# Two attention stages: diagonal blocks cleared by GpSimd in the first, four heads side by side with sums by GpSimd in the second

## The reference

```python
# layer 0 (latent keys and values, 8 values per head, 32 shared rotary rows); layer 1 (latent of 32, no rotary)
scores = q @ k.T * scale              # per batch and head, 1024 x 1024
scores = where(key <= query, scores, -inf)
probs = exp(scores - max) / sum(exp(scores - max))
x = x + (probs @ v) @ W_o
```

## Time and profile before

| | us |
|---|---|
| median of 3 runs | 3160.7 |
| lowest, highest | 3154.9, 3165.1 |
| the profiled execution | 3168.4 |
| span of its trace | 3166.7 |

### The profile page before, as it was taken

The page is one execution under the profiler, slowest core; times in us unless marked ns, Lnnn a source line. Parts: engine busy times, 40 slices in busy tenths (PEclk is TensorE's granted clock), DMA queues, the critical chain, the costliest instruction groups (busy, mean ns, idle before and its releaser), DMA issues. The chain is left out here.

```text
span 3166.7 us, 46665 instructions
## 1 busy us (share of the span) xinstructions
PE 2361.7 (75%) x13512; PEld 1225.4 (39%) x13512; DVE 1743.7 (55%) x5508; ACT 1241.0 (39%) x1983; POOL 488.8 (15%) x524
## 2 busy tenths in 40 slices
PE   4559999999956328866999999999677292877382
PEld 1114344343334126532443434444254271554262
DVE  4656666666344886265665655666365324576223
ACT  2405455555534644553444444444222141343141
POOL 1400000000003000032000000000043463033554
PEclk9759999999977659877999999999888596988686
DMA  4272444443030000233122121121120152000144
GB/s 130 76 144 45 86 76 85 86 85 60 11 103 3 1 8 28 64 110 109 44 57 54 45 55 42 48 64 37 60 83 21 52 142 81 3 4 15 40 138 129
DMA packets 177903, 199.81 MB, mean 63 GB/s; under 512 B 36384, under 2 KB 117920, under 8 KB 177568
## 3 DMA queue, kind: packets, MB, share of 16 engines
q1 hardware_dynamic: 160000, 173.72, 22.1%
q0 software_dynamic: 9216, 19.02, 1.8%
q10 hardware_dynamic: 8448, 4.20, 0.4%
HBM read 127.09 MB, written 69.76 MB: 62 GB/s over the span
## 5 line engine op out<-in xcount | busy, mean ns | idle before, releaser
L910 ACT ACTIVATE at_probs<-at_score 128x1024 f32<-128x1024 f32 (+7 forms) x1024 | 655.2, 652 | 872.8 <-PE at_score L835 539.1
L935 DVE CUSTOM_DVE_ANT_0 at_masked<-at_mx,g_maskw 128x512 bf16<-128x512 f32 (+3 forms) x1024 | 483.4, 486 | 180.9 <-PE at_mx L801 177.6
L801 PE MATMUL at_mx<-at_K,at_Q 96*128 96x512 bf16 (+7 forms) x1536 | 467.0, 344 | 119.0 <-DVE at_mpart L935 40.9
L833 PE MATMUL at_score<-at_Q,at_K 96*128 96x512 bf16 (+7 forms) x1536 | 504.1, 332 | 28.9 <-issue 14.3
L835 PE MATMUL at_score<-at_Q,at_K 98*128 98x512 bf16 (+7 forms) x1536 | 507.2, 331 | 0.0
L931 DVE TENSOR_REDUCE at_mpart<-at_mx 128x1 f32<-128x512 f32 x512 | 353.8, 691 | 265.3 <-PE at_mx L801 245.1
L855 PE MATMUL at_outp<-at_probs,at_vop 128*32 128x512 f32 (+6 forms) x3072 | 445.2, 497 | 0.0
L801 PEld LDWEIGHTS at_mx<-at_K,at_Q 120*128 120x128 bf16 (+1 forms) x1536 | 148.4, 98 | 440.3 <-DVE at_mpart L935 198.6
L833 PEld LDWEIGHTS at_score<-at_Q,at_K 120*128 120x128 bf16 (+1 forms) x1536 | 149.8, 98 | 339.3 <-issue 183.1
L1025 POOL MEMSET n_spread<- 16x128 f32 (+1 forms) x2 | 0.7, 356 | 1541.0 <-POOLq L636 1541.0
L838 PE MATMUL at_score<-g_maskkq,g_identb 128*128 128x128 bf16 x1024 | 225.3, 220 | 0.0
(11 more groups left out here) (467 smaller groups left out, 3408.6 us busy)
## 6 DMA issues: line engine op xcount, KB each, us to landing
at_Q<-q SPq DMA_DIRECT2D x192, 128.0 KB, 3.0
at_Q<-qr SPq DMA_DIRECT2D x72, 256.0 KB, 5.9
at_K<-kr SPq DMA_DIRECT2D x72, 256.0 KB, 6.9
q<-p_pieces SPq DMA_DIRECT2D x40, 384.0 KB, 3.3
at_K<-k SPq DMA_DIRECT2D x168, 64.0 KB, 2.1
buf<-g_zeros SPq DMA_DIRECT2D x32, 325.0 KB, 5.0
o<-at_osb SPq DMA_DIRECT2D x64, 128.0 KB
n_oc<-o SPq DMA_DIRECT2D x8, 1024.0 KB, 5.0
```

Of the source, the lines that this page charges most:

```text
L801: pe.matmul(bank[:, 0:hi - lo], Q0[0:R, g % 4, j, qt * P:(qt + 1) * P], K0[0:R, g % 4, j % KG, lo:hi], start=True, stop=True).then_inc(s_m ...
L833: pe.matmul(bank, K0[0:R0, g % 4, j % KG, kb * P:(kb + 1) * P], Q0[0:R0, g % 4, j, lo:hi], start=True, stop=False)
L910: act.activation(probs[:, kb % 2, j, kb * P:T], src, ACT.Exp, scale=cf.scale).then_inc(s_exp, 1)
L935: dve.tensor_tensor_reduce(masked[:, u % 2, 0:w], mx[:, u % 2, 0:w], k.maskw[:, CH - w:CH], 1.0, NEG, ALU.add, ALU.max, mpart[:, part, j, ...
```

## The change

For both stages: `Cfg` gets `clear_probs` (true in the first attention) and `pool_sums` (true where `d == M`, which is the second attention with its new `G=4, M=32`).

First attention: TensorE no longer adds the mask to the diagonal block. GpSimd sets the entries above the diagonal of each 128x128 diagonal block of `probs` to zero after the exponential, and `values` waits for that.

Second attention: 16 steps of 4 heads in place of 32 of 2. The values fill all 32 columns, so there is no column of ones. GpSimd adds the `probs` of key blocks 0 to 6 in f32 into `acc` (24 additions and one that copies, per step), `probs` becomes a ring of 3, and TensorE multiplies `acc` and the last block with ones into the two `mx` banks at the step's end (`sums`), from which VectorE copies them to `lsb`. The mask of the second attention stays on TensorE.

```diff
+        self.clear_probs = bool(SR)
+        self.pool_sums = d == M
...
-    MU = 12 * G + 2
+    MU = 12 * G + SU + 2
+    NBP = 3 if SUMS else 2
+    ADDED = 6
...
+        def add_probs(b, g):
+            pool = nc.gpsimd
+            n = b * GN + g
+            for kb in range(1, ADDED + 1):
+                for j in range(G):
+                    pool.wait_ge(s_exp, n * U + kb * G + j + 3)
+                    if kb == 1 and j == 0:
+                        pool.wait_ge(s_mx, earlier_sums(b, g))
+                        pool.tensor_tensor(acc[:, :, 0:P], probs[:, 0, :, 0:P],
+                                           k.zeros[:, 0:G * P].rearrange("p (j t) -> p j t", t=P), ALU.add).then_inc(s_acc, 1)
+                    if kb > 1:
+                        pool.wait_ge(s_acc, added(n, kb - 1, j))
+                    so_far = probs[:, 0, j, P:T] if kb == 1 else acc[:, j, kb * P:T]
+                    pool.tensor_tensor(acc[:, j, kb * P:T], so_far, probs[:, kb % NBP, j, kb * P:T],
+                                       ALU.add).then_inc(s_acc, 1)
...
+            def clear_diagonals(b, g):
+                n = b * GN + g
+                for kb in range(QT):
+                    for j in range(G):
+                        part = probs[:, kb % NBP, j, kb * P:(kb + 1) * P]
+                        pool.wait_ge(s_exp, n * U + kb * G + j + 3)
+                        pool.sem_inc(s_ppassed, 1)
+                        pool.affine_select(out=part, in_=part, compare_op=ALU.is_ge, fill=0.0, base=0,
+                                           pattern=[[1, P]], channel_multiplier=-1).then_inc(s_dg, 1)
...
-                    diag = lo == kb * P
+                    diag = lo == kb * P and not cf.clear_probs
...
+                if cf.clear_probs:
+                    pe.wait_ge(s_dg, n * U + (kb + 1) * G)
...
+            def sums(b, g):
+                u = sum_at(b, g)
+                pe.wait_ge(s_acc, added(b * GN + g, ADDED, G - 1))
+                for half in range(2):
+                    pe.wait_ge(s_mxf, u + half + 1)
+                    for j in range(G):
+                        out = mx[M * j:M * (j + 1), half, :]
+                        last = pe.matmul(out, ones[:], acc[:, j, half * CH:(half + 1) * CH], start=True, stop=(half == 0))
+                    if half == 1:
+                        for j in range(G):
+                            last = pe.matmul(mx[M * j:M * (j + 1), half, CH - P:CH], ones[:],
+                                             probs[:, (QT - 1) % NBP, j, T - P:T], start=False, stop=True)
+                    last.then_inc(s_mx, 1)
...
-                    act.wait_ge(s_pv, n * 8 + kb - 1 + NPC)
+                    act.wait_ge(s_pv, n * 8 + (kb - 1 if kb < 2 or not SUMS else max(kb - 2, 0)) + NPC)
...
+                        if SUMS and kb == 0:
+                            act.wait_ge(s_acc, added(n - 1, ADDED, j))
+                        if SUMS and kb >= 3:
+                            act.wait_ge(s_acc, added(n, max(kb - 3, 1), j))
...
+                for half in range(2 if SUMS else 0):
+                    dve.wait_ge(s_mx, sum_at(b, g) + half + 1)
+                    dve.tensor_copy(lsb[:, g % 2, half * CH:(half + 1) * CH], mx[:, half, :]).then_inc(s_mxf, 1)
...
-        cf = Cfg(G=2, M=64, HR=0, SR=0, d=LD, scale=0.125, k_per_head=False)
+        cf = Cfg(G=4, M=32, HR=0, SR=0, d=LD, scale=0.125, k_per_head=False)
```

More of the change, by code:

```diff
@@ L628, in attention @@
     U = QT * G
-    MU = 12 * G + 2
+    SUMS = cf.pool_sums
+    SU = 2 if SUMS else 0
+    MU = 12 * G + SU + 2
+    NBP = 3 if SUMS else 2
+    ADDED = 6
+    AU = 1 + ADDED * G
     NARROW = {5: [3], 6: [2, 1], 7: [0]}
@@ L648, in attention @@
         osb = c.sb("osb", [P, 2, T])
+        if SUMS:
+            acc = c.sb("acc", [P, G, T])
+            ones = c.sb("ones", [P, 32])
+            lsb = c.sb("lsb", [P, 2, T])
         masked = c.sb("masked", [P, 2, CH], BF16)
@@ L663, in attention @@
         s_ms, s_passed = c.sem("shift_stored"), c.sem("sync_passed")
-        s_dpassed = c.sem("vector_passed")
+        s_dpassed, s_ppassed = c.sem("vector_passed"), c.sem("pool_passed")
+        s_dg = c.sem("diagonal_cleared")
+        s_acc = c.sem("probs_added")
+        STORES = 2 if SUMS else G + 1
         block = st.enter_context(nc.Block())
@@ L703, in ahead, with sum_at, earlier_sums, added @@
             return b, g
+        def sum_at(b, g):
+            n = b * GN + g
+            if ahead(b, g, 2):
+                return (n + 2) * MU + SUM_U
+            return NB * GN * MU + (2 if g == GN - 1 else 0)
+        def earlier_sums(b, g):
+            n = b * GN + g
+            if ahead(b, g, 1):
+                return (n + 1) * MU + SUM_U + 2
+            return NB * GN * MU + 2
+        def added(n, kb, j):
+            return (n + 1) * AU + 1 + (kb - 1) * G + j + 1
         def over_batches(eng, step):
@@ L752, in store @@
                 wait(s_oev, b * GN + g + 2)
+                if SUMS:
+                    sp.dma_start(o_scr[ds(g * G * d, G * d), ds(first_token(b), T)], osb[:, g % 2, :]).then_inc(s_os[g % 2], 16)
+                    wait(s_mxf, sum_at(b, g) + 4)
+                    sp.dma_start(l_scr[ds(g * G, G), ds(first_token(b), T)],
+                                 lsb[0:(G - 1) * M + 1:M, g % 2, :]).then_inc(s_os[g % 2], 16)
+                    return
                 for j in range(G):
@@ L783, in _ @@
             pool.memset(K1[SHIFT_ROW:SHIFT_ROW + 2, :, :, :], 1.0).then_inc(s_set, 1)
+            if SUMS:
+                pool.wait_ge(s_set, 1)
+                pool.memset(ones[:], 1.0).then_inc(s_set, 2)
+                pool.sem_inc(s_acc, AU)
+                over_batches(pool, add_probs)
+                return
             pool.wait_ge(s_set, 1)
@@ L804, in max_units, with turn_max @@
                 return u
-            def turn_max(b, g, u):
+            def turn_max(b, g, u, off=0):
                 n = b * GN + g
@@ L893, in step @@
                 values(b, g, QT - 1)
+                if SUMS:
+                    sums(b, g)
             over_batches(pe, step)
@@ L916, in _, with reduce_units @@
         def _(dve):
-            dve.sem_inc(s_mxf, 2)
+            dve.sem_inc(s_mxf, 2 + 2 * SU)
             dve.sem_inc(s_oev, 1)
-            dve.sem_inc(s_os[0], 16 * (G + 1))
-            dve.sem_inc(s_os[1], 16 * (G + 1))
-            def reduce_units(b, g, parts, u):
+            dve.sem_inc(s_os[0], 16 * STORES)
+            dve.sem_inc(s_os[1], 16 * STORES)
+            def reduce_units(b, g, parts, u, off=0):
                 n = b * GN + g
@@ L939, in reduce_units, with finish_max @@
                 return u
-            def finish_max(b, g, u):
+            def finish_max(b, g, u, off):
                 n = b * GN + g
-                dve.wait_ge(s_mxf, n * MU + u + 2)
+                dve.wait_ge(s_mxf, n * MU + u + 2 + off)
                 dve.tensor_tensor(mpart[:, 0, :, 4:8], mpart[:, 0, :, 4:8], mpart[:, 1, :, 4:8], ALU.max).then_inc(s_mc, 1)
@@ L962, in copy_turned, with wide_maxima @@
                     u += 1
-            def wide_maxima(b, g):
-                u = reduce_units(b, g, WIDE, NARROW_U)
-                finish_max(b, g, u)
-                copy_turned(b, g, u)
+            def wide_maxima(b, g, off=0):
+                u = reduce_units(b, g, WIDE, WIDE_AT, off)
+                finish_max(b, g, u, off)
+                copy_turned(b, g, u, off)
             def values(b, g):
@@ L975, in _ @@
             values(0, 0)
-            reduce_units(0, 0, NARROW, 0)
-            wide_maxima(0, 0)
-            reduce_units(0, 1, NARROW, 0)
+            reduce_units(0, 0, NARROW, 0, 2 * SU)
+            wide_maxima(0, 0, SU)
+            reduce_units(0, 1, NARROW, 0, SU)
             def step(b, g):
```

45 lines of the change are left out of this document (28 added, 17 removed).

## The result

| | before | changed kernel |
|---|---|---|
| median | 3160.9 us | 3237.8 us (3221.9 to 3247.3) |
| ratio, 95% interval | | 1.0238 (1.0218 to 1.0259), slower |
| profiled execution, span | 3166.7 us | 3245.5 us |
| first exponential to end of last copy, first attention | 646.3 us | 645.0 us |
| the same, second attention (with the copies of the sums) | 786.6 us | 845.0 us |

The account below looks back on a forecast made before the run. TensorE, helped by VectorE, was taken to set the pace. Second attention -40.2 us and first -8 us bring 3168.4 us to 3120 profiled, 3112 us as median; 8-in-10 range 3065 to 3165 us.

Parts of the forecast that it names:

- What GpSimd does to VectorE: Second attention: GpSimd's additions block `finish_max`, stalling TensorE 2.8 us in each of 15 steps, 42 us.
- the forecast's picture: In `finish_max`, the first instruction waits for the rest of one addition, the three others for a whole one: 5.6 us.
- Steps as in the first attention: Second attention: its 16 steps take the first attention's 646.3 us in place of 786.6, a gain of 140.3 us.
- sums on TensorE 2.1 us: Second attention, step's end: the products with ones cost 2.1 us in each of 16 steps, 33.6 us.
- lead-in: Before the second attention's first score: maxima of twice the heads cost 21.3 us more, longer query loads 1.8 us.
- Does GpSimd keep up?: Second attention: GpSimd's additions take 32.4 us a step at 2.26 ns a column, about level with TensorE.
- the upper row: GpSimd's additions: five in a row took 6.06 us, 2.37 ns a column, which would give 33.9 us a step.
- 0.5 us late at the most: Second attention: without the stall, GpSimd's additions end at most 0.5 us after TensorE's last values of a step.
- First attention, -8 us: First attention: dropping the mask products saves 0.5 us a step, 8 us, with 0 and 28 as ends; clearing costs nothing.
- no contention: Rival, second attention: VectorE's tiny instructions slip in between additions, saving the 42 us; 3078 us, chance 0.17.
- GpSimd is the bound and the kernel gets slower: Rival, second attention: TensorE waits at `sums` for the last addition; up to 3211 us at the slowest row, chance 0.25.
- The forecast's own test: Changed trace: TensorE idle ahead of `sums` means wrong price per column; idle at neither `sums` nor `turn_max`, wrong contention.

Follow-up runs that it names:

- filled stall: Changed kernel with 36 products of 512 columns, results unread, on TensorE ahead of its wait for `finish_max`; 3218.0 us, ratio 1.0182.
- thin additions: Changed kernel with each of GpSimd's 24 additions of a step cut to its first 32 columns; 3081.1 us (one execution).
- PSUM form: Changed kernel with `finish_max` as three instructions, the first a reduction, in place of four, intermediate values in a free PSUM bank; 3121.5 us, ratio 0.9869.
- second part alone: Changed kernel without the clearing: first attention's mask stays a product on TensorE, only the second attention is changed; 3233.9 us, ratio 1.0216.
- halved additions: Changed kernel with each of GpSimd's 24 additions of a step cut into two instructions of half the columns; 3282.1 us (one execution).
- the maximum with its result in PSUM: Changed kernel with `finish_max` in three instructions through PSUM, the first a maximum of two SBUF operands in place of a reduction; 3225.7 us (one execution).

## Why the prediction was wrong

**The step that failed is the one headed "What GpSimd does to VectorE", and in it the length of the wait.** Who blocks whom is right: `finish_max` is blocked by GpSimd's additions, since its operands lie in SBUF, and TensorE idles ahead of `turn_max`. The moment is right too (chain 23.9 us into the step, forecast 24.0), and in one chain of 15 so is the size. But the first instruction was priced at the rest of one addition, 0.45 us, with 3.8 us as the upper bound of the whole stall; in 14 chains of 15 it waited 10.4 us, for the end of GpSimd's run. The term is 15 x 2.8 = 42 us, and 117.0 were measured.

The rows that it rested on the earlier trace rows are true, and the trace before has more of their kind. In it VectorE instructions with two SBUF operands were held while another addition was still to come, and all 20 got in at the first boundary: 12 L460 (six of them in runs of two additions, as in rows 9, six in runs of five), and 8 L1293. VectorE in the run of five of rows 6, then the third, fourth and fifth of its additions:

```profile
1376.13 1.48 DVE L1293 TENSOR_TENSOR p_rest<-p_lat,p_pieces 32x512 f32<-32x512 f32 x1 [0.32 <-ACT p_pieces L1249]
...
1377.93 0.72 DVE L460 SCALAR_TENSOR_TENSOR p_shift<-p_mv,p_rstd 128x4 f32<-128x4 f32 x1
```

```profile
1375.91 1.16 POOL L1309 TENSOR_TENSOR p_pieces<-p_rest,p_pieces 128x512 bf16<-128x512 f32 x1
1377.03 1.60 POOL L1309 TENSOR_TENSOR p_pieces<-p_rest,p_pieces 128x512 bf16<-128x512 f32 x1
1378.59 1.14 POOL L1309 TENSOR_TENSOR p_pieces<-p_rest,p_pieces 32x512 bf16<-32x512 f32 x1
```

L1293 has 0.94 us of the third addition in front of it, about what L1055 has of its own, and gets in behind it; the fourth addition is held in turn (1.60 us). L460 gets in behind the fourth. So the old trace spoke for the forecast's picture, and the fault was to take what held in one stage for a bound in another. What makes the difference is open. A bound from the other side was to be had: whatever stands in front of GpSimd without waiting for this chain, which is the rest of block 3 (0.9 + 3 x 1.5 us) and block 4 (4 x 1.22), 10.3 us.

The 121.7 us that are missing in the second attention:

| term | forecast | measured | from |
|---|---|---|---|
| stall ahead of `turn_max` | 42 | 117 | waits of the changed kernel |
| clock behind the stall | 0 | 20 to 35 | filled stall: difference of the medians, and 14 held steps x 2.5 us |
| GpSimd's tail in the last step | 0 | about 11 | last copy of the sums 9.3 us behind the copy-out, 1.9 with thin additions; that copy-out 34.0 us after the step's first exponential, 30.1 with them (ScalarE waits 6.0 us for GpSimd in that step, 1.3 with them) |
| sum of the differences | | 106 to 121 of 122 | |

What is left, 1 to 16 us, I did not take apart.

- *Steps as in the first attention, sums on TensorE 2.1 us, lead-in:* right. Last values to next scores take 2.05 us; from the first L877 to the first exponential it is 46.5 us, 21.5 more than before, forecast 21.3 and 1.8.
- *The clock* is missing from the forecast altogether, though it knew of a stall. Even the stall of the forecast's size, 2.67 us, was followed by slower products (L911 with 384 columns 0.53 us, 0.33 at the full clock, in the rows above), and its step is 5.1 us longer than the same one with thin additions (50.5 against 45.5 us, both at the turn of the loop). This alone would have made 42 us some 76.
- *Does GpSimd keep up?* Not quite: it works from 6.85 to 40.85 us into an undisturbed step, 34.0 us or 2.37 ns a column, where I took 2.26. That this is the price of the upper row is chance: the 6.06 us there hold the 0.45 us by which the fourth addition was held. The others start 1.12 us apart, and additions of 512 columns with f32 operands 1.22 us, so with f32 operands, named as the open part, an addition costs some 9% more. TensorE's values end at 39.5. "0.5 us late at the most" was 0.4 to 1.9 us in 14 steps of the PSUM form and 5.0 and 5.6 us in the last two. In the changed kernel the stall covers this, as the forecast said; without the stall it is the next limit (29.1 us of waits; the second attention of the PSUM form takes 721.5 us, with thin additions 678.3).
- *First attention, -8 us:* wrong, and with the other sign; measured +3.5 us (+0.6 to +6.3). Plain steps do get 0.2 to 0.6 us shorter (40.1 and 40.0 in place of 40.3 and 40.6), but VectorE's reductions take the place of the product. A few steps are 1 us longer in some executions (with a dip of the clock in them), and the two at the turn of the loop 0.6 us (46.7 in place of 46.1).
- *The rivals:* "no contention" (3078) is what the thin additions give (3081), but it wasn't the case here. "GpSimd is the bound and the kernel gets slower" had the right sign and engine but the wrong path: the time is lost at `turn_max`, not at `sums`. The forecast's own test said so in advance: idle time at `turn_max` speaks for contention, at `sums` for the price.

## What to carry to other kernels

Before GpSimd is given long work in a row, list VectorE's instructions in that stretch with two SBUF inputs or with a copy or scaling from SBUF to SBUF, and bound the wait of each by the whole of GpSimd's queue, not by one instruction. A chain on the critical path can be written with reductions and a PSUM end instead; here that cost nothing. Price a stall of TensorE with the half-speed stretch behind it. And a wait seen in one stage, even 20 times of 20, is a size and not a bound for another: put the worst case that the instruction order allows beside it.

## What the runs showed of the hardware

- In the second attention a blocked VectorE instruction is mostly held for the whole back-to-back run of GpSimd: 10.4 us over seven boundaries between additions, 12.6 us over more than twice as many of half the length. It either gets in at the first boundary (1.0 us) or at none: of 75 first links with two SBUF sources in five kernels (the changed one, its second part alone, filled stall, halved additions, and the maximum with its result in PSUM), 7 got in at the first and 68 waited for the end of the run; none lies between. In the stages ahead of the attentions 20 of 20 got in at the first. What decides it is open; in the four kernels with whole additions all came 0.52 to 0.67 us into one. The Trainium skill (SBUF — State Buffer, "Who interferes with whom") has the lock for the whole instruction; these runs show longer.
- The lock works both ways: the addition behind the boundary at which L1293 got in took 1.60 us in place of 1.15, 8 times of 8.
- Once VectorE has got in, the following links of the old chain get in too, one addition each (1.45 to 1.47 us, all 12 links of 4 such chains).
- TensorE's clock went to 0.50 for 5.1 us of work behind 8.2 us of idle, and fell as well behind 2.7 us; with 7.9 us of idle products in the stall it stayed at 1.00.
